# Wider, double-buffered conversion of the attention weights on two engines, and key transposes moved from the group stage to the chunk stage

## The chip, the cores and the metric

The program runs on the 8 cores of one Trainium2 chip, one sequence of the batch on each core, without communication between them. The metric is the device time of the slowest core in microseconds. The kernel before has a median of 5968.18 us over two runs (5965.78 and 5970.58).

## The reference

Each core computes one macaron layer for 2048 tokens of width 1024: half a feed-forward block, an attention block, and half a feed-forward block with the same weights again. Cut to what matters:

```python
x = x + 0.5 * ffn(layernorm(x), w_gate, w_up, w_down)
x = x + attn(layernorm(x), Wq, Wk, Wv, Wo, Wg1, Wg2, gamma, beta)
x = x + 0.5 * ffn(layernorm(x), w_gate, w_up, w_down)

def ffn(x, ...):      # every operand goes through a blockwise fp4 quantize-dequantize
    return fp4_linear(silu(fp4_linear(x, w_gate)) * fp4_linear(x, w_up), w_down)

def attn(x, ...):     # linear attention: no softmax, causal mask by multiplication
    q, k = lrpe(x @ Wq), lrpe(x @ Wk)            # silu, then rotary
    energy = einsum('bnhd,bmhd->bhnm', q, k) * tril
    out = einsum('bhnm,bmhd->bnhd', energy, x @ Wv)
    out = out * sigmoid(x @ Wg1 @ Wg2)
    return (layernorm(out) * gamma + beta) @ Wo
```

## The kernel before, in words

The program has four stages, with a barrier of all engines and all DMA counters (emit_phase_barrier, line 395) after the first, second and third.

**Weight preparation.** The activations x go into the SBUF tensor R (128 x 16384 fp32) once and stay there. The feed-forward weights are loaded, quantized on VectorE (DVE), transposed on TensorE (PE) into the PSUM tensor psW, evacuated by ScalarE (ACT) into evacW, and stored by DMAs that GpSimd (POOL) issues, into DRAM scratch tensors s_wgT, s_wuT, s_wdT. Then the four attention weights (q, k, v, o; 1024 x 1024 fp32 each) are only converted to bf16. This is the loop at lines 361 to 393: for each of four matrices and each of DK = 8 row blocks, SyncE (SP) loads a block of 128 x 1024 fp32 (512 KB) into wldA or wldB by turns (line 373), ACT casts it into one half of evacW (buf[:, 0:DM], 128 x 1024), and POOL issues the store of 256 KB to s_wq, s_wk, s_wv or s_wo (line 389). Two things set the order. The load waits for `sac.n`, the last ACT instruction emitted, so the load of block k waits for the cast of block k-1. The cast calls wait_stores, which waits for every store emitted so far (counters sgw, sgwd, sga), so cast k waits for store k-1 although it writes the other half of evacW:

```python
y.wait_ge(sac.h, sac.n)          # load k: the cast of block k-1
...
s.wait_ge(slot.h, ldm)           # cast k: its load
wait_stores(s)                   #         and all stores so far
```

**Feed-forward 1 and 2** (emit_ffn_call) read the scratch weights and work on four tiles of 128 tokens at a time. The diff does not touch them.

**Attention** (emit_attn). Work goes by groups g of GT = 2 chunks of 128 tokens, 8 groups in all; wbufA has three slots for weights, loaded by SP. The order in which instructions are emitted is the order of each engine's queue. For each group: sections(g); mixing(2g); epilogue(2g-1); o_load; emit_gate; mixing(2g+1); epilogue(2g).

sections(g) normalizes and transposes two tiles into xn_fm, then projects q and k in 8 steps each. A step is: PE matmuls into psA (line 748), ACT silu into qs_b, PE rotation matmul into psB (line 770), ACT copy into qp_b, and four DVE instructions that write qh or kh. After the last step of k, PE transposes kh for each of the two chunks, 16 instructions of 64 x 128 (line 817) into the one PSUM tensor psD, and DVE copies psD out (first chunk to ktm_sb, second chunk to the reused wkA). Then PE computes v for both chunks (line 852), with an ACT copy into v_g after each, and the small product with Wg1 (line 874).

mixing(c) runs four blocks of four heads: PE scores into psC (line 952), DVE multiplies by the mask into sTm, PE accumulates the output in psA from sTm and from the running state Sb (lines 979 and 983). Then PE multiplies the transposed keys with v_g into psB (line 1000), and DVE adds that to the fp32 state S32 and writes Sb. epilogue(c) is gate, layer norm, transposes, output projection (line 1099) and residual.

Each ACT block of instructions is preceded by an ACT_TABLE_LOAD, whatever its function. Vector and scalar instructions go through a helper, so that all have line 137; they are told apart by their tiles.

Of the kernel before, what the change touches and what calls it, by code (L numbers as in the profile page):

```python
# [9 lines left out]
BF16 = mybir.dt.bfloat16  # L10
# [15 lines left out]
GT = 2  # L26
# [11 lines left out]
def build_program():  # L38
# [70 lines left out]
    sga = Ctr("sga")  # L109
    sfg = [Ctr("sfg0"), Ctr("sfg1")]  # L110
# [7 lines left out]
    dma_ctrs = [ssu, slw[0], slw[1], sgw, sgwd, sga, sfg[0], sfg[1],  # L118
# [146 lines left out]
    def wait_stores(e):  # L265
        for ctr in (sgw, sgwd, sga):
            if ctr.n > 0:
                e.wait_ge(ctr.h, ctr.n)

    with ExitStack() as wes:  # L270
# [4 lines left out]
        evacW = WSB("evacW", [128, 2048], BF16)  # L275
# [3 lines left out]
        with nc.psum_tensor("psW", [128, 2048], BF16) as psW:  # L279
# [82 lines left out]

            for nm in ("q", "k", "v", "o"):
                dsrc, ddst = {"q": (dwq, s_att["q"]), "k": (dwk, s_att["k"]),
                              "v": (dwv, s_att["v"]), "o": (dwo, s_att["o"])}[nm]
                for k in range(DK):
                    buf = wldA if (k % 2 == 0) else wldB
                    pp = k % 2
                    slot = slw[k % 2]

                    def _(y, k=k, buf=buf, dsrc=dsrc):
# [7 lines left out]
                    def _(s, buf=buf, ldm=ldm, pp=pp, slot=slot):  # L379
# [4 lines left out]
                    S(_)  # L384
                    am = sac.n

                    def _(g, k=k, am=am, pp=pp, ddst=ddst):
                        g.wait_ge(sac.h, am)
                        g.dma_start(out=ddst[k * 128:(k + 1) * 128, :],
                                    in_=evacW[:, pp * 1024:(pp + 1) * 1024]).then_inc(sga.h, 16)  # L390
                    G(_)
                    sga.n += 16
            wprep_marks["attn"] = sga.n
# [243 lines left out]
    def emit_attn(rwaits):  # L637
        with ExitStack() as aes:
# [23 lines left out]
            with nc.psum_tensor("psA", [128, 2048], F32) as psA, \  # L662
# [10 lines left out]
                ktm_rd = {0: 0, 1: 0}  # L673
                ktm_b = {0: ktm_sb, 1: wkA[:, 0:512].bitcast(BF16)}
# [3 lines left out]
                def sections(g):  # L678
# [44 lines left out]
                    for nm, wp in (("q", 0), ("k", 1)):  # L723
                        def _(y, nm=nm, wp=wp, g=g, slot=sat[wp]):
                            y.wait_ge(spe.h, wsl_rd[wp])
                            if g == 0:
                                y.wait_ge(sga.h, wprep_marks["attn"])
# [79 lines left out]

                    qk_now = sdv.n
                    ctx["ktm_e"] = {}
                    for cl in range(GT):  # L810
                        def _(t_, cl=cl, qk_now=qk_now):
                            t_.wait_ge(sdv.h, qk_now)
                            t_.wait_ge(sdv.h, rs["psD_v"])
                            t_.wait_ge(sac.h, rs["psD_s"])
                            last = None
                            for hc in range(H):
                                last = t_.transpose(
                                    psD[:, hc * 64:(hc + 1) * 64],
                                    kh[:, hc * GTOK + cl * 128: hc * GTOK + (cl + 1) * 128],
                                    identb[0:64, 0:64])  # L820
                            spe.inc(last)
                        T(_)
                        ktt_m = spe.n

                        def _(v, cl=cl, ktt_m=ktt_m):
# [3 lines left out]
                        V(_)  # L829
                        ctx["ktm_e"][cl] = sdv.n  # L830
                        rs["psD_v"] = sdv.n
# [104 lines left out]
                def mixing(c):  # L936
# [55 lines left out]
                    def _(t_, cl=cl, ctx=ctx):  # L992
                        t_.wait_ge(sdv.h, ctx["ktm_e"][cl])
# [3 lines left out]
                        kts = ktm_b[cl]  # L997
                        last = None
                        for hc in range(H):
                            last = t_.matmul(psB[0:64, hc * 64:(hc + 1) * 64],  # L1000
                                             kts[:, hc * 64:(hc + 1) * 64],
# [5 lines left out]
                    ktm_rd[cl] = sup_m  # L1007
# [197 lines left out]
```

## Time and profile before

| what | us |
|---|---|
| median of the runs | 5968.18 |
| device time of the profiled execution | 5960.58 |
| span of its slowest core (core 5) | 5959.0 |
| spans of the eight cores | 5950.6 to 5959.0 |
| first load of the attention weights issued, and the feed-forward's first DVE instruction | 739.70, 972.62 |
| feed-forward 1, attention, feed-forward 2 (rounded edges) | 972 to 2690, 2690 to 4330, 4330 to 5959 |
| busy: PE, DVE, ACT, POOL | 1845.4, 2508.9, 1646.7, 384.2 |

Positions are microseconds from the start of the span of core 5. "Busy" is the time in which an engine executes. A row of the timeline reads: start, duration, engine, line, operation, output<-inputs, count, and in brackets the idle time ahead of it with what ended it. PEclk is the granted TensorE clock as a share of 2.4 GHz, so 0.50 is 1.2 GHz and 1.00 is 2.4 GHz.

### The profile page before, as it was taken

To read this page: it belongs to the slowest core of one execution; us is meant where nothing else is said; L and a number is where in the kernel's file an instruction comes from. 1 tells how busy PE (TensorE), PEld (TensorE's weight loads), DVE (VectorE), ACT (ScalarE), POOL (GpSimd) and SP (SyncE) were. 2 spreads that over 40 slices of the span, in tenths; PEclk is the share of its full clock that TensorE was granted. 3 is DMA by queue.
4 is the path that set the end of the run, shared out by engine and by line. 5 is a ranking of instruction groups with operands and counts; after the bars stand their busy time and mean duration, and the time that the engine had idled before them with its cause. 6 is when DMAs were issued, how large, how long until landed. Compare 5 with 4: busy or idle time off the path is not lost.

```text
span 5959.0 us, 36038 instructions; the slowest of 8 cores (5950.6 to 5959.0 us)
## 1 busy us (share of the span) xinstructions
PE 1845.4 (31%) x9264; PEld 924.1 (16%) x9264; DVE 2508.9 (42%) x3398; ACT 1646.7 (28%) x1718; POOL 384.2 (6%) x605
## 2 busy tenths in 40 slices
PE   0010100433333334423333333333323424344333
PEld 0000000211111111212211211211111212121111
DVE  7798602444535535322222222222246355354452
ACT  1222233222212212153342342242222223121220
POOL 3454500000000000000000000000000000000000
PEclk9999999776676666755555555555556766666667
DMA  4122132102020021110101101101011210220212
GB/s 148 67 76 78 60 109 85 53 25 67 25 64 29 25 64 53 36 57 29 49 23 43 57 15 43 57 15 43 29 34 48 64 28 25 64 53 27 65 25 92
DMA packets 209652, 304.60 MB, mean 51 GB/s; under 512 B 29808, under 2 KB 128112, under 8 KB 208432
## 3 DMA queue, kind: packets, MB, share of 16 engines
q1 hardware_dynamic: 184544, 256.98, 14.6%
q0 software_dynamic: 24912, 45.32, 2.1%
q8 instruction: 84, 1.38, 0.1%
q14 instruction: 112, 0.92, 0.1%
HBM read 268.11 MB, written 34.08 MB: 51 GB/s over the span
## 4 chain that ended last, share of the span: by engine, by line
DVE 29%; PE 27%; ACT 18%; issue 10%; DMA 9%; POOL 5%; DVEq 1%; ACTq 0%; POOLq 0%; SPq 0%
ACT L137 11%; PE psg L524 5%; PE psu L527 5%; PE psA L748 4%; DVE q_cF L137 4%; DMA wdb<-s_wdT 3%; PE psd L617 3%; DVE hb L137 3%; DVE q_iF L137 3%; DVE q_rF L137 3%; DVE q_bmF L137 3%; DVE wkD L137 2%; DVE btB L137 2%; POOL s_wdT L354 2%; ACT evacW L137 2%
## 5 line engine op out<-in xcount | busy, mean ns | idle before, releaser
L137 ACT ACT_TABLE_LOAD x815 | 1045.6, 1283 | 4204.5 <-PE pstB L572 1042.2
L524 PE MATMUL psg<-wgb,xq 128*128 128x512 bf16 (+1 forms) x1536 | 572.5, 381 | 39.3 <-ACT xq L137 21.7
L527 PE MATMUL psu<-wub,xq 128*128 128x512 bf16 (+1 forms) x1536 | 569.9, 380 | 0.0
L572 PE MATMUL pstB<-identb,btB 128*128 128x128 bf16 x704 | 90.2, 305 | 1158.1 <-DVE btB L137 1158.1
L137 DVE TENSOR_TENSOR hb<-wkA,psu 128x512 f32<-128x512 f32 (+1 forms) x192 | 123.5, 643 | 675.1 <-ACT wkA L137 675.1
L617 PE MATMUL psd<-wdb,hq 128*128 128x512 bf16 x1408 | 351.4, 398 | 106.9 <-DMA wdb<-s_wdT 85.3
L137 DVE TENSOR_TENSOR btB<-qs_b,cosr 128x256 bf16<-128x256 bf16 x128 | 37.4, 292 | 737.0 <-ACT qp_b L137 737.0
L1145 POOL DMA_DIRECT2D out<-R x16 | 8.4, 533 | 4953.7 <-DVE R L137 4953.7
L748 PE MATMUL psA<-xn_fm,wbufA 128*128 128x256 bf16 x1024 | 238.8, 413 | 277.4 <-ACT qp_b L137 255.0
L464 PE MATMUL pstA<-identb,btA 128*128 128x128 bf16 x256 | 32.4, 305 | 919.0 <-DVE btA L137 919.0
L333 PE MATMUL psW<-identb,wqb 128*128 128x128 bf16 x528 | 67.1, 306 | 665.3 <-ACT evacW L137 445.8
L572 PEld LDWEIGHTS pstB<-identb,btB 128*128 128x128 bf16 x704 | 67.4, 136 | 1184.7 <-issue 1184.7
L137 DVE SCALAR_TENSOR_TENSOR R<-psd,R 128x4096 f32<-128x4096 f32 x8 | 35.4, 4425 | 468.1 <-PE psd L617 468.1
L524 PEld LDWEIGHTS psg<-wgb,xq 128*128 128x128 bf16 x1536 | 156.9, 102 | 217.1 <-issue 80.0
L748 PEld LDWEIGHTS psA<-xn_fm,wbufA 128*128 128x128 bf16 x1024 | 132.2, 138 | 360.3 <-issue 311.4
L527 PEld LDWEIGHTS psu<-wub,xq 128*128 128x128 bf16 x1536 | 156.3, 102 | 169.2 <-issue 31.3
L617 PEld LDWEIGHTS psd<-wdb,hq 128*128 128x128 bf16 x1408 | 131.8, 101 | 324.7 <-issue 209.9
L464 PEld LDWEIGHTS pstA<-identb,btA 128*128 128x128 bf16 x256 | 24.7, 137 | 928.2 <-issue 928.2
L137 DVE TENSOR_REDUCE st_s<-R 128x4 f32<-128x4096 f32 (+1 forms) x9 | 52.6, 5842 | 269.0 <-DMA s_wo<-evacW 267.7
L137 DVE TENSOR_TENSOR sTm<-psC,mask 128x512 bf16<-128x512 f32 x64 | 44.2, 691 | 268.3 <-PE psC L952 267.4
L333 PEld LDWEIGHTS psW<-identb,wqb 128*128 128x128 bf16 x528 | 50.9, 137 | 681.2 <-issue 681.2
L137 DVE TENSOR_TENSOR q_cF<-q_iF,q_cF 128x1024 bf16<-128x1024 f32 (+1 forms) x128 | 148.2, 1158 | 13.7 <-DVE q_cF L137 0.5
(131 smaller groups left out, 3709.3 us busy)
## 6 DMA issues: line engine op xcount, KB each, us to landing
wdb<-s_wdT SPq DMA_DIRECT2D x176, 256.0 KB, 2.6
wgb<-s_wgT SPq DMA_DIRECT2D x320, 128.0 KB, 3.0
wub<-s_wuT SPq DMA_DIRECT2D x320, 128.0 KB, 3.1
wbufA<-s_wq SPq DMA_DIRECT2D x64, 256.0 KB, 7.8
wbufA<-s_wk SPq DMA_DIRECT2D x64, 256.0 KB, 9.1
wbufA<-s_wv SPq DMA_DIRECT2D x64, 256.0 KB, 4.5
wbufA<-s_wo SPq DMA_DIRECT2D x64, 256.0 KB, 5.4
R<-x POOLq DMA_DIRECT2D x16, 512.0 KB, 19.4
```

The source lines that it names most:

```text
L137: instr = f(*a, **kw)
L333: last = t.transpose(psW[:, pp * 1024 + s * 128: pp * 1024 + (s + 1) * 128], wqb[:, qb * FFI + (g0 + s) * 128: qb * FFI + (g0 + s + 1) * 128],
L354: g.dma_start(out=ddstT[c0 + s * 128: c0 + (s + 1) * 128, jcol * 128:(jcol + 1) * 128], in_=evacW[:, pp * 1024 + s * 128: pp * 1024 + (s + ...
L464: last = t_.transpose(pstA[:, pp * 1024 + k * 128: pp * 1024 + (k + 1) * 128], btA[:, pp * DM + k * 128: pp * DM + (k + 1) * 128], identb[:])
L524: t_.matmul(psg[:, pp * 512: pp * 512 + mw], lhs, wgbuf[:, wp * 4096 + k * 512: wp * 4096 + k * 512 + mw], start=(k == 0), stop=(k == DK - 1))
L527: last = t_.matmul(psu[:, pp * 512: pp * 512 + mw], lhs, wubuf[:, wp * 4096 + k * 512: wp * 4096 + k * 512 + mw], start=(k == 0), stop=(k ...
L572: last = t_.transpose(pstB[:, qpp * 1024 + sb * 128: qpp * 1024 + (sb + 1) * 128], btB[:, qpp * DM + sb * 128: qpp * DM + (sb + 1) * 128], ...
L617: last = t_.matmul(psd[:, j * 1024 + hf * 512: j * 1024 + (hf + 1) * 512], lhs, wdbuf[:, wp * DM + hf * 512: wp * DM + (hf + 1) * 512], st ...
L748: last = t_.matmul(psA[:, pp * 512: pp * 512 + GTOK], wbufA[:, wp * 8192 + k * 1024 + m * 128: wp * 8192 + k * 1024 + (m + 1) * 128], xn_f ...
L1145: g.dma_start(out=dout[t * TILE:(t + 1) * TILE, :], in_=Rt(t)).then_inc(sgo.h, 16)
```

## The change

Two parts.

**Attention weights.** The loop takes two row blocks at a time: 4 x 4 items instead of 4 x 8. A load carries 128 x 2 x 1024 fp32 (1 MB), a cast 128 x 2048, a store 512 KB; evacW grows from 2048 to 4096 columns, so each of two slots has its own 2048. Even items are cast by ACT as before, odd ones by DVE. The load of item ii waits for the cast of item ii-2 alone (the first two wait for the last DVE quantization). The cast waits for its load and for the stores of its own slot: the counter sga is split into sga and sga2. SP still issues all loads and POOL all stores, in order.

**Key transposes.** The transposes of kh and the DVE copy of psD leave sections(g) and go into mixing(c), between the last output matmul and the matmul that updates the state. Both chunks use ktm_sb; the second buffer and its waits are gone.

```diff
-        evacW = WSB("evacW", [128, 2048], BF16)
+        evacW = WSB("evacW", [128, 4096], BF16)
...
-                for k in range(DK):
-                    buf = wldA if (k % 2 == 0) else wldB
-                        y.wait_ge(sac.h, sac.n)
-                        y.dma_start(out=buf[:, 0:DM],
-                                    in_=dsrc[k * 128:(k + 1) * 128, :]).then_inc(slot.h, 16)
-                        s.wait_ge(slot.h, ldm)
-                        wait_stores(s)
-                        sac.inc(s.copy(evacW[:, pp * 1024:(pp + 1) * 1024],
-                                       buf[:, 0:DM]))
...
+                for k0 in range(0, DK, 2):
+                    ii = it2[0]
+                    it2[0] += 1
+                    buf = wldA if (ii % 2 == 0) else wldB
+                    pp = ii % 2
+                    sst = sgat[pp]
+                    use_v = (pp == 1)
+                        prev = cp_marks.get(ii - 2)
+                        if prev:
+                            y.wait_ge(prev[0].h, prev[1])
+                        else:
+                            y.wait_ge(sdv.h, sdv.n)
+                        y.dma_start(
+                            out=buf[:, 0:2 * DM].rearrange("p (t c) -> p t c", c=DM),
+                            in_=dsrc[k0 * 128:(k0 + 2) * 128, :]
+                            .rearrange("(t p) c -> p t c", p=128)).then_inc(slot.h, 16)
+                    def cpwaits(e, ldm=ldm, slot=slot, sst=sst):
+                        e.wait_ge(slot.h, ldm)
+                        for ctr in (sgw, sgwd, sst):
+                            if ctr.n > 0:
+                                e.wait_ge(ctr.h, ctr.n)
+                    if use_v:
+                            sdv.inc(v.tensor_copy(
+                                evacW[:, pp * 2048:(pp + 1) * 2048],
+                                buf[:, 0:2 * DM]))
+                    else:
+                            sac.inc(s.copy(
+                                evacW[:, pp * 2048:(pp + 1) * 2048],
+                                buf[:, 0:2 * DM]))
+                        g.wait_ge(cm[0].h, cm[1])
+                        g.dma_start(
+                            out=ddst[k0 * 128:(k0 + 2) * 128, :]
+                            .rearrange("(t p) c -> p t c", p=128),
+                            in_=evacW[:, pp * 2048:(pp + 1) * 2048]
+                            .rearrange("p (t c) -> p t c", c=DM)).then_inc(sst.h, 16)
```

In sections(g) this goes (with the 16 transposes of each chunk ahead of it):

```diff
-                            v.wait_ge(spe.h, ktt_m)
-                            v.wait_ge(spe.h, ktm_rd[cl])
-                            sdv.inc(v.tensor_copy(ktm_b[cl][:], psD[:]))
```

In mixing(c) this comes, after the last output matmul:

```diff
+                        t_.wait_ge(sdv.h, ctx["qk_m"])
+                        t_.wait_ge(sdv.h, rs["psD_v"])
+                        t_.wait_ge(sac.h, rs["psD_s"])
+                        last = None
+                        for hc in range(H):
+                            last = t_.transpose(
+                                psD[:, hc * 64:(hc + 1) * 64],
+                                kh[:, hc * GTOK + cl * 128: hc * GTOK + (cl + 1) * 128],
+                                identb[0:64, 0:64])
+                        spe.inc(last)
...
+                        v.wait_ge(spe.h, ktm_m)
+                        sdv.inc(v.tensor_copy(ktm_sb[:], psD[:]))
```

What SP's queue holds at the start of the attention weights, before (wldA and wldB are the load buffers; sac counts ACT's instructions, sdv DVE's):

```order
L373 DMA wldA<-wq 128x1024 [waits sac]
L375 UNCONDITIONAL_BRANCH
L373 DMA wldB<-wq 128x1024 [waits sac]
L375 UNCONDITIONAL_BRANCH
L373 DMA wldA<-wq 128x1024 [waits sac]
```

and now:

```order
L385 DMA wldA<-wq 128x2x1024 [waits sdv]
L389 UNCONDITIONAL_BRANCH
L385 DMA wldB<-wq 128x2x1024 [waits sdv]
L389 UNCONDITIONAL_BRANCH
L385 DMA wldA<-wq 128x2x1024 [waits sac]
L389 UNCONDITIONAL_BRANCH
L385 DMA wldB<-wq 128x2x1024 [waits sdv]
```

A load is twice as large, and loads to wldB now follow DVE instead of ACT.

On PE, at the end of the k projection of a group, before (line 770 is the last rotation matmul, line 852 the v projection):

```order
L770 MATMUL psB<-qs_b,p128t 128x256 [waits sac,sdv]
L822 UNCONDITIONAL_BRANCH
L817 MATMUL psD<-identb,kh 128x64 [waits sdv,sac]
L817 MATMUL psD<-identb,kh 128x64 x15
L822 UNCONDITIONAL_BRANCH
L817 MATMUL psD<-identb,kh 128x64 [waits sdv,sac]
L817 MATMUL psD<-identb,kh 128x64 x15
L857 UNCONDITIONAL_BRANCH
L852 MATMUL psA<-wbufA,xn_fm 128x512 [waits sat0,sac,sdv]
```

and now (lines 801 and 858 are the same two matmuls):

```order
L801 MATMUL psB<-qs_b,p128t 128x256 [waits sac,sdv]
L863 UNCONDITIONAL_BRANCH
L858 MATMUL psA<-wbufA,xn_fm 128x512 [waits sat0,sac,sdv]
L858 MATMUL psA<-wbufA,xn_fm 128x512 x15
```

The v projection follows the rotation matmul directly. At the end of a chunk's mixing, before (line 983 is the last output matmul, line 1000 the state update):

```order
L979 MATMUL psA<-v_g,sTm 128x64
L983 MATMUL psA<-Sb,qh 128x64
L1005 UNCONDITIONAL_BRANCH
L1000 MATMUL psB<-v_g,ktm_sb 64x64 [waits sdv,sac]
L1000 MATMUL psB<-v_g,ktm_sb 64x64 x15
```

and now (lines 989 and 1026):

```order
L985 MATMUL psA<-v_g,sTm 128x64
L989 MATMUL psA<-Sb,qh 128x64
L1009 UNCONDITIONAL_BRANCH
L1004 MATMUL psD<-identb,kh 128x64 [waits sdv,sac]
L1004 MATMUL psD<-identb,kh 128x64 x15
L1031 UNCONDITIONAL_BRANCH
L1026 MATMUL psB<-v_g,ktm_sb 64x64 [waits sdv,sac]
L1026 MATMUL psB<-v_g,ktm_sb 64x64 x15
```

The 16 transposes now stand between the output matmuls and the state update, once per chunk; the DVE copy that stands between them waits for the one and releases the other.

## Rows read from the trace of the kernel before

**Rows 1.** The page: the chain that ended last, by engine, and the granted clock by slices

```profile
DVE 29%; PE 27%; ACT 18%; issue 10%; DMA 9%; POOL 5%; DVEq 1%; ACTq 0%; POOLq 0%; SPq 0%
PEclk9999999776676666755555555555556766666667
```

**Rows 2.** Timeline, two steps of the attention weights' conversion

```profile
745.04 1.28 ACT L137 ACT_TABLE_LOAD   x1 [5.41 <-DMA s_wdT<-evacW]
746.33 1.04 ACT L137 CAST evacW<-wldA 128x1024 bf16<-128x1024 f32 x1
...
751.91 1.28 ACT L137 ACT_TABLE_LOAD   x1 [4.54 <-DMA s_wq<-evacW]
...
972.62 4.42 DVE L137 TENSOR_REDUCE st_s<-R 128x4 f32<-128x4096 f32 x1 [267.67 <-DMA s_wo<-evacW]
```

**Rows 3.** Busy time by stretch: engines, then granted clock, DMA share, GB/s

```profile
10.00:40.00 30.00, 0.00 (x0) 0.00 (x0) 27.58 (x24) 0.00 (x0) 5.23 (x10) 1.00 1.00 333
745.00:972.00 227.00, 0.00 (x0) 0.00 (x0) 0.00 (x0) 74.50 (x64) 17.29 (x32) 1.00 0.36 109
```

**Rows 4.** DMA issues of the whole run: queue, count, KB each, median us to landing

```profile
wldA<-wgate SPq DMA_DIRECT2D x6, 1024.0 KB, 6.1
...
s_wgT<-evacW POOLq DMA_DIRECT2D x176, 32.0 KB, 1.8
```

**Rows 5.** Tile R before 745 us: the 16 loads of x, 512 KB each

```profile
L245 POOL DMA_DIRECT2D R<-x x16: 546/563/667, 1.6 to 9.5; - x16
...
DMA to landing us min/median/max: 11.3/19.4/30.4
```

**Rows 6.** Groups by shape, feed-forward weights (100 to 740) and attention (2690 to 4330)

```profile
L137 DVE TENSOR_SCALAR q_rW<-wldA 128x2048 bf16<-128x2048 f32 x10 | 12.3, 1227 | 1.1
...
L137 ACT CAST qp_b<-psB 128x256 bf16<-128x256 f32 x114 | 42.5, 372 | 1.3
```

**Rows 7.** Timeline, end of the k projection of the first group and its v projection

```profile
2696.73 0.37 ACT L137 CAST qp_b<-psB 128x256 bf16<-128x256 f32 x1
...
2698.13 0.68 DVE L137 TENSOR_TENSOR kh<-btB 64x256 bf16<-64x256 bf16 x2
...
2699.16 1.01 PE L817 MATMUL psD<-identb,kh 64*128 64x64 bf16 x16 [3.92 <-DVE kh L137]
2700.41 0.69 DVE L137 COPY ktm_sb<-psD 128x1024 bf16<-128x1024 bf16 x1 [1.61 <-PE psD L817]
...
2701.36 1.00 PE L817 MATMUL psD<-identb,kh 64*128 64x64 bf16 x16 [1.19 <-DVE ktm_sb L137]
...
2702.29 5.31 PE L852 MATMUL psA<-wbufA,xn_fm 128*128 128x512 bf16 x16
```

**Rows 8.** Timeline, end of the first chunk's mixing

```profile
2733.28 1.06 PE L1000 MATMUL psB<-v_g,ktm_sb 128*64 128x64 bf16 x16
2734.58 1.21 DVE L137 TENSOR_TENSOR S<-S,psB 64x1024 f32<-64x1024 f32 x1 [2.96 <-PE psB L1000]
```

**Rows 9.** Busy time by stretch: columns as in rows 3, around v, and by stage

```profile
2699.00:2705.60 6.60, 5.25 (x40) 2.94 (x41) 1.38 (x2) 0.00 (x0) 0.00 (x0) 0.50 0.00 0
2705.60:2708.00 2.40, 2.00 (x9) 0.72 (x7) 0.00 (x0) 0.26 (x1) 0.00 (x0) 0.97 0.00 0
972.00:2690.00 1718.00, 603.74 (x2871) 285.83 (x2871) 758.94 (x1094) 470.50 (x498) 0.00 (x0) 0.68 0.16 46
4330.00:5959.00 1629.00, 578.21 (x2760) 271.39 (x2760) 736.89 (x1047) 391.88 (x398) 8.39 (x16) 0.67 0.17 48
```

**Rows 10.** Timeline, GpSimd's issue of eight stores of s_wdT, twice

```profile
527.72 4.25 POOL L354 DMA_DIRECT2D s_wdT<-evacW  x8 [12.59 <-ACT evacW L137]
...
558.37 7.80 POOL L354 DMA_DIRECT2D s_wdT<-evacW  x8 [8.37 <-ACT evacW L137]
560.04 1.63 DVE L137 TENSOR_SCALAR q_iW<-q_iW 128x2816 int32<-128x2816 int32 x1
```

**Rows 11.** Tile v_g: the copies of the v projection, two per group

```profile
L137 ACT CAST v_g<-psA x16: 1012/1012/1013, 2709.0 to 4247.7; 128x1024 bf16<-128x1024 f32 x16
```

More of the change, by code:

```diff
@@ L109, in build_program @@
     sga = Ctr("sga")
+    sga2 = Ctr("sga2")
+    sgat = [sga, sga2]
     sfg = [Ctr("sfg0"), Ctr("sfg1")]
@@ L265, in wait_stores @@
     def wait_stores(e):
-        for ctr in (sgw, sgwd, sga):
+        for ctr in (sgw, sgwd, sga, sga2):
             if ctr.n > 0:
@@ L361, in build_program @@
                 wprep_marks[name] = sst.n
+            it2 = [0]
+            cp_marks = {}
             for nm in ("q", "k", "v", "o"):
@@ L365, in build_program, with _ @@
                               "v": (dwv, s_att["v"]), "o": (dwo, s_att["o"])}[nm]
-                for k in range(DK):
-                    buf = wldA if (k % 2 == 0) else wldB
-                    pp = k % 2
-                    slot = slw[k % 2]
-                    def _(y, k=k, buf=buf, dsrc=dsrc):
-                        y.wait_ge(sac.h, sac.n)
-                        y.dma_start(out=buf[:, 0:DM],
-                                    in_=dsrc[k * 128:(k + 1) * 128, :]).then_inc(slot.h, 16)
+                for k0 in range(0, DK, 2):
[3 more added lines that the diff above has]
+                    pp = ii % 2
+                    slot = slw[pp]
+                    sst = sgat[pp]
+                    use_v = (pp == 1)
+                    def _(y, k0=k0, buf=buf, dsrc=dsrc, ii=ii, slot=slot):
+                        prev = cp_marks.get(ii - 2)
[7 more added lines that the diff above has]
+                            .rearrange("(t p) c -> p t c", p=128)).then_inc(slot.h, 16)
                     Y(_)
@@ L391, in build_program, with _ @@
-                    G(_)
-                    sga.n += 16
-            wprep_marks["attn"] = sga.n
+                    def cpwaits(e, ldm=ldm, slot=slot, sst=sst):
[4 more added lines that the diff above has]
+                    if use_v:
+                        def _(v, pp=pp, buf=buf):
+                            cpwaits(v)
+                            sdv.inc(v.tensor_copy(
+                                evacW[:, pp * 2048:(pp + 1) * 2048],
+                                buf[:, 0:2 * DM]))
+                        V(_)
+                        cp_marks[ii] = (sdv, sdv.n)
+                    else:
+                        def _(s, pp=pp, buf=buf):
+                            cpwaits(s)
+                            sac.inc(s.copy(
+                                evacW[:, pp * 2048:(pp + 1) * 2048],
+                                buf[:, 0:2 * DM]))
+                        S(_)
+                        cp_marks[ii] = (sac, sac.n)
@@ L395, in emit_phase_barrier @@
+                    sst.n += 16
+            wprep_marks["attn"] = (sgat[0].n, sgat[1].n)
     def emit_phase_barrier():
@@ L726, in _ @@
                             if g == 0:
-                                y.wait_ge(sga.h, wprep_marks["attn"])
+                                y.wait_ge(sga.h, wprep_marks["attn"][0])
+                                y.wait_ge(sga2.h, wprep_marks["attn"][1])
                             for k in range(DK):
@@ L806, in sections @@
                     wsl_rd[1] = projpe["k"]
[L808 to L825, printed above, removed]
-                            v.wait_ge(spe.h, ktt_m)
-                            v.wait_ge(spe.h, ktm_rd[cl])
-                            sdv.inc(v.tensor_copy(ktm_b[cl][:], psD[:]))
-                        V(_)
-                        ctx["ktm_e"][cl] = sdv.n
-                        rs["psD_v"] = sdv.n
                     def _(y, g=g, slot=sat[0]):
@@ L992, in _ @@
                     def _(t_, cl=cl, ctx=ctx):
-                        t_.wait_ge(sdv.h, ctx["ktm_e"][cl])
+                        t_.wait_ge(sdv.h, ctx["qk_m"])
[8 more added lines that the diff above has]
+                        spe.inc(last)
+                    T(_)
+                    ktm_m = spe.n
+                    def _(v, ktm_m=ktm_m):
+                        v.wait_ge(spe.h, ktm_m)
+                        sdv.inc(v.tensor_copy(ktm_sb[:], psD[:]))
+                    V(_)
+                    ktme_m = sdv.n
+                    rs["psD_v"] = ktme_m
+                    def _(t_, cl=cl, ktme_m=ktme_m, ctx=ctx):
+                        t_.wait_ge(sdv.h, ktme_m)
                         t_.wait_ge(sac.h, ctx["v_m"])
@@ L1000, in _ @@
                             last = t_.matmul(psB[0:64, hc * 64:(hc + 1) * 64],
-                                             kts[:, hc * 64:(hc + 1) * 64],
+                                             ktm_sb[:, hc * 64:(hc + 1) * 64],
                                              v_g[:, cl * DM + hc * 64: cl * DM + (hc + 1) * 64],
```

15 lines of the change are left out of this document (3 added, 12 removed).

## The prediction

> **What bounds the kernel now.** I read the page's chain first [rows 1]: DVE 29%, PE 27%, ACT 18%, DMA 9%, POOL 5%. No engine is the bound alone; the end is set by hand-overs, so what a step costs is its length on the chain of its stage. The 9% of DMA and 5% of POOL are transfers and their issue that something waited for. The timeline says where: after the last store of the feed-forward weights every step of the attention weights' conversion has one shape [rows 2]. Two 512 KB blocks never overlap. ACT idles 4.54 us for the store of the block before, loads its table (1.28), casts (1.04), and only then are the next load and this block's store issued (SP waits for the cast, front section). 32 such steps fill the time from 745.04 to the barrier at about 972.4, 227.4 us or 7.1 us each; DVE waits 267.67 us for the end of it [rows 2]. All of it is on the chain, and in it the DMA engines are busy only 36% [rows 3]: the stage is bound by latency, not by bytes. In attention each group is a serial hand-over between PE, ACT and DVE, so single pieces of 1 or 2 us count there as well.
>
> **The attention weights.** The bytes are the same: 32 x 512 KB read, 32 x 256 KB written, 25.2 MB.
>
> Removed: 32 serial steps, 227.4 us.
>
> Put in their place: 8 rounds, in each of which slot A (ACT) and slot B (DVE) do a load of 1 MB, a cast of 128 x 2048 and a store of 512 KB. The pieces:
> - DVE cast: the same form of output, input and width took 1.23 us as a tensor_scalar [rows 6].
> - ACT cast: 1.04 us for 1024 columns [rows 2], 0.37 for 256 [rows 6], so 0.88 ns per column and 1.94 us for 2048; with the table load 3.2 us.
> - DMA at full load: 109 GB/s at a share of 0.36 is 303 GB/s at a share of 1; a stretch of loads alone, with every DMA engine busy, moved 333 [rows 3]. The first has the mix of loads and stores that stays, in rows of 1024 elements as before, so I take 303.
> - Landing: a load of 1 MB took 6.1 us, a store of 32 KB 1.8 [rows 4], so about 1.8 us of a transfer is fixed.
>
> By latency alone slot A's round would be 6.1 + 3.2 + 0.1 for the hand-over = 9.4 us. By bytes a round is 3.15 MB / 303 GB/s = 10.4 us. The bytes decide, if the two slots' transfers fill each other's gaps. They do if transfers of one queue land one after the other rather than together. The 16 loads of x say so: issued within 8 us, they landed after 11.3 to 30.4 us, not all at the end [rows 5]. So A's load lands about halfway through a round, ACT casts for 3.2 us while B's transfers still flow, and B's cast runs while A's new ones do.
>
> Sum from 745.04 on: the first two loads are there already (they may now start after the last quantization, 267.67 us before 972.62, at 705). ACT's first cast with its issue takes 3.2 + 0.7 = 3.9 us. Then the rest of the bytes, 25.2 less 2.1 of the first two loads, is 23.1 MB at 303 GB/s, 76 us. I add 0.9 us in each of 7 rounds for gaps that the overlap leaves, half of the fixed 1.8, and 3 us at the end for the last DVE cast and the landing of its store. 3.9 + 76 + 6 + 3 = 89 us, so 138 are saved. The early pair of loads, 2.1 MB or some 7 us of full DMA, meets one or two stores of s_wdT that are on the chain. That costs between nothing and all of its 7 us; I take 2, since the stores' packets come between the loads' ones: net 136.
>
> Bounds: at 333 GB/s with no gaps it is 3.9 + 69 + 3 = 76, a saving of 151. With no overlap at all between a round's transfers and its casts, a round is 10.4 + 1.8 + 3.2 + 0.5 = 15.9, and 7 rounds with start and end 111 + 3.9 + 7 = 122, a saving of 105. I stay near the first since the landing rows speak for overlap.
>
> **The key transposes out of sections.** The first v matmul started at 2702.29 to 2702.36, behind both chunks' transposes and a DVE copy [rows 7]. Its other waits are older: the last qp_b copy ended at 2697.10, and PE follows an engine by 0.26 us (the copy to ktm_sb ended at 2701.10, the next transposes began at 2701.36 [rows 7]). The qp_b copy's end is 2696.73 + 0.37. So v starts at 2697.36, 5.0 us earlier, in each of 8 groups: 40 us. What is late next is v itself; DVE finishes kh at 2698.81 as before [rows 7], long before the scores need it.
>
> One loss is hidden in it. In this stretch PE ran at a granted 0.50 (1.2 GHz) and came to 0.97 (2.4 GHz) at 2705.6, about halfway through the first v batch, after 6.4 us in which transposes and v followed each other [rows 9]. Without transposes ahead, the rise may come no earlier in the batch or later. The batch took 5.31 us [rows 7]; all at 1.2 GHz, 16 x 512 columns is 6.8. So it costs between 0 and 1.5 us in each group. I take 0.4, nearer to the first, since v is itself most of the work ahead of the rise: 3 us in all.
>
> **The key transposes into mixing.** Before, the update matmuls followed the output matmuls at once (2733.28) and DVE waited 2.96 us for them with nothing else queued [rows 8]. Now PE transposes, DVE copies, PE goes on: 2701.36 - 2699.16 = 2.2 us by the very same pieces [rows 7], all in line. Behind the waiting copy in DVE's queue stands the state update, then the epilogue; nothing passes it. In 16 chunks this is 35 us. Nothing stands beside it that could hide it, and the other marks that the transposes wait for (psD, kh) are old by then, so I give it 0.2 us either way: 32 to 38 us.
>
> Attention in sum: -40 + 3 + 35 = -2 us, between -8 and +10.
>
> **Sum.** 5960.6 (the profiled execution) - 136 - 2 = 5822.6. The median of the runs shown stands 7.6 us above that execution, 0.13%; I take part of this in and say 5825 us, 2.4% below the median. A measurement of this kernel can tell about 2% from no change, that is 119 us, so faster than 5849 counts as faster.
>
> **Rivals.**
> - *Lockstep.* The two slots' transfers share the engines and land together, so both casts stand in the open: the upper bound above, a saving of 105 and 2, 5854 us. For it: both slots' first transfers are issued within a microsecond. Against it: the landing times of x. Chance 0.10.
> - *The descriptor stall.* While DVE worked on SBUF operands with one tensor input, eight store issues of GpSimd took 7.80 us instead of 4.25 [rows 10], so an issue can be held by a DVE instruction of that kind. The new DVE cast is one, and its 1.23 us can hold the store of the other slot once a round: 8 x 1.2 = 10 us, 5835 us. Chance 0.10. The Trainium skill's page "SBUF — State Buffer" (section "Who interferes with whom") says that DVE casts in a two-port mode and GpSimd's descriptor writes exclude each other for the whole instruction. The trace agrees with a slowdown, 7.80 against 4.25, and by that rule this rival's 10 us would be the ceiling. Before the change no DVE work ran in this stage.
> - *v does not move.* Something other than the transposes holds the v projection, for instance a wait that the trace hides behind them. Then the 40 us do not come and 35 are added: 5865 us. Against it: SP asks for v's weights once the q projection is done, eight steps of the k projection earlier. Chance 0.03.
> - *The clock is paid back.* PE is idle through the whole conversion with its clock granted in full [rows 3], the slices fall to 0.7 and less right behind it [rows 1], and in the feed-forward stages it is granted 0.68 and 0.67 with 604 + 578 = 1182 us of PE busy time [rows 9]. If a shorter rest lowers the grant, the feed-forwards pay. It decides from 1182 x (0.68 / c - 1) = 138, c = 0.61. At 0.50 in both stages it costs 425 us: 6248 us, slower. Against it: the grant in feed-forward 2, long after any rest, is the same as in feed-forward 1. Chance 0.01.
>
> **How the numbers follow.** The forecast has 0.76. Faster by over 2% holds for the forecast and the stall; the worst of the forecast's own spread: 0.76 + 0.10 = 0.86. Within 2%, with lockstep and v: 0.10 + 0.03 = 0.13. Slower: 0.01. The range is 5804 to 5853: the low end is the bound of 151 with attention at -6, the high end just reaches the lockstep case's edge.
>
> **What would show it.** In the changed profile the stretch from the first attention-weight cast to the first instruction of feed-forward 1 should be 85 to 95 us long with a DMA share of 0.85 to 0.95, and successive ACT casts 10.5 to 12 us apart. Lockstep would show spacings near 16 and a share near 0.65. The stall would show as store issues of GpSimd over 1.5 us long. In attention the v matmuls should begin 0.3 us after the last qp_b copy, the update matmuls 2.2 us after the last output matmul, and the group's period, (4247.7 - 2709.0 less the 6.3 between a group's two copies) / 7 = 219 us [rows 11], should change by less than 1 us. The granted clock of both feed-forward stages should stay at 0.67 to 0.68; if it falls below 0.61 the forecast is wrong in sign. If the period of a group grows by 4 us or more, the v step failed.

## The result, and the profile after

The changed kernel has a median of 5848.14 us (5838.01 to 5886.59, 9 runs) against 5969.09 us before (8 runs): a ratio of 0.9805, with a 95% interval of 0.9774 to 0.9836. It is faster, by 1.6 to 2.3%; whether by more than the 2% that the forecast named, the interval leaves open. The forecast was 5825 us, in a range of 5804 to 5853, so the time lies inside the range, 23 us above the point and 5 us below the upper end. In the profiled execution cores 4 to 7 ran for 267 to 420 us of the feed-forward stages at a granted clock of 0.81, a level that cores 0 to 3 never show there and that four cores of the run with the old conversion show too, so all comparisons below are of cores 0 to 3, unless others are named.

First the answer to [rows 1], the page of the slowest core after:

```profile
DVE 29%; PE 28%; ACT 18%; issue 10%; DMA 8%; POOL 5%; DVEq 1%; ACTq 0%; SPq 0%; POOLq 0%
```

The shares hardly move, although over 120 us are gone; a chain by engine does not find a stage. The times between fixed points of the program do. They are means over cores 0 to 3, from the first DVE instruction of feed-forward 1 and from the first and last ACT copy of v:

| stretch, us | before | after |
|---|---|---|
| start to feed-forward 1 | 965.1 | 839.7 |
| feed-forward 1, to the first copy of v | 1736.4 | 1734.0 |
| attention, first to last copy of v | 1538.8 | 1539.4 |
| from there to the end | 1713.5 | 1717.9 |

The whole gain, 125 us, lies ahead of feed-forward 1. Attention did not change. The two other stages differ by -2 and +4.

The timeline of core 0 of the changed kernel, two rounds of the conversion, answers to [rows 2]:

```profile
755.45 1.28 ACT L139 ACT_TABLE_LOAD   x1 [8.91 <-DMA s_wq<-evacW]
756.74 1.90 ACT L139 CAST evacW<-wldA 128x2048 bf16<-128x2048 f32 x1
757.41 1.23 DVE L139 CAST evacW<-wldB 128x2048 bf16<-128x2048 f32 x1 [12.80 <-DMA s_wq<-evacW]
758.73 0.37 SPq L385 DMA_DIRECT2D wldA<-wk  x1
759.18 1.42 POOL L418 DMA_DIRECT2D s_wq<-evacW  x2 [10.66 <-ACT evacW L139]
759.60 0.37 SPq L385 DMA_DIRECT2D wldB<-wk  x1
767.37 1.28 ACT L139 ACT_TABLE_LOAD   x1 [8.72 <-DMA s_wq<-evacW]
```

The two casts cost what was worked out (1.90 and 1.23 us). But both fall into the same 3 us, and all four transfers of a round are issued within 2 us of each other. ACT then waits 8.7 us, and not for its load: the row says that a store ended the wait. The DMA issues of that core from 744 us on show which lands first (columns: queue, count, KB, median us to landing):

```profile
s_wk<-evacW POOLq DMA_DIRECT2D x4, 512.0 KB, 8.9
wldA<-wv SPq DMA_DIRECT2D x2, 1024.0 KB, 6.2
wldB<-wv SPq DMA_DIRECT2D x2, 1024.0 KB, 10.2
```

Slot A's load is there after 6.2 us, but its cast writes the buffer that the store of two items back still reads, and that takes 8.9. All seven waits of ACT between its casts end with a store. Slot B waits for its load, 10.2, in five of its seven rounds, and for its store in the other two, of which the rows above show one. So the slots run nearly in step. The busy time of the same core in a stretch of the conversion answers to [rows 3] (columns as there; the last three are granted clock, DMA share, GB/s):

```profile
760.00:825.00 65.00, 0.00 (x0) 0.00 (x0) 6.14 (x5) 15.90 (x10) 8.09 (x11) 1.00 0.77 264
```

The DMA engines are busy 77% (68 to 77% over the eight cores), where 85 to 95% was expected and 36% was the share before. 264 GB/s at a share of 0.77 is 343 GB/s at full share.

In attention, the end of a chunk's mixing answers to [rows 7, 8]:

```profile
2595.60 1.04 PE L1004 MATMUL psD<-identb,kh 64*128 64x64 bf16 x16
2596.81 0.69 DVE L139 COPY ktm_sb<-psD 128x1024 bf16<-128x1024 bf16 x1 [2.76 <-PE psD L1004]
...
2597.97 1.03 PE L1026 MATMUL psB<-v_g,ktm_sb 128*64 128x64 bf16 x16 [1.34 <-DVE ktm_sb L139]
2599.25 1.21 DVE L139 TENSOR_TENSOR S<-S,psB 64x1024 f32<-64x1024 f32 x1 [1.75 <-PE psB L1026]
```

The update stands 2.37 us behind the transposes (2.2 forecast). At the other end, the first v batch follows the last rotation copy (2565.27 + 0.37) by 0.25 us, as forecast:

```profile
2565.27 0.37 ACT L139 CAST qp_b<-psB 128x256 bf16<-128x256 f32 x1
...
2565.89 5.23 PE L858 MATMUL psA<-wbufA,xn_fm 128*128 128x512 bf16 x16 [2.11 <-ACT qp_b L139]
```

So both steps happened, 5.0 us gained per group and 2.37 lost per chunk, and over 8 groups and 16 chunks the sum is 40 against 38. The period of a group is 219.0 us as a mean over all cores, as before.

### The profile page after: what moved, and what is told of

Same layout as the page of the kernel before. It is cut to its first block, busy times and chain, and to the rows that moved or that the text cites. A ratio compares the mean times of both kernels' runs of the same rounds, so it can differ in the third digit from the quotient of the medians.

```text
span 5885.1 us, 35854 instructions; the slowest of 8 cores (5828.3 to 5885.1 us)
## 1 busy us (share of the span) xinstructions
PE 1909.0 (32%) x9264; PEld 936.8 (16%) x9264; DVE 2518.3 (43%) x3406; ACT 1597.8 (27%) x1670; POOL 379.1 (6%) x589
## 4 chain that ended last, share of the span: by engine, by line
DVE 29%; PE 28%; ACT 18%; issue 10%; DMA 8%; POOL 5%; DVEq 1%; ACTq 0%; SPq 0%; POOLq 0%
ACT L139 11%; PE psg L556 6%; PE psu L559 6%; PE psA L779 4%; DVE q_cF L139 4%; PE psd L649 4%; DMA wdb<-s_wdT 4%; DVE hb L139 3%; DVE q_iF L139 3%; DVE q_rF L139 3%; DVE q_bmF L139 3%; DVE wkD L139 2%; DVE btB L139 2%; POOL s_wdT L356 2%; DVE q_ivF L139 2%
## 5 line engine op out<-in xcount | busy, mean ns | idle before, releaser
L556 PE MATMUL psg<-wgb,xq 128*128 128x512 bf16 (+1 forms) x1536 | 591.7, 393 | 38.8 <-ACT xq L139 21.3
L559 PE MATMUL psu<-wub,xq 128*128 128x512 bf16 (+1 forms) x1536 | 588.8, 392 | 0.0
L649 PE MATMUL psd<-wdb,hq 128*128 128x512 bf16 x1408 | 377.6, 422 | 101.4 <-DMA wdb<-s_wdT 80.7
L139 DVE TENSOR_REDUCE q_bmF<-hb 128x64 f32<-128x1024 f32 (+1 forms) x96 | 108.5, 1131 | 102.2 <-PE pstB L604 99.7
```

Source lines behind the costliest of these rows:

```text
L139: instr = f(*a, **kw)
L556: t_.matmul(psg[:, pp * 512: pp * 512 + mw], lhs, wgbuf[:, wp * 4096 + k * 512: wp * 4096 + k * 512 + mw], start=(k == 0), stop=(k == DK - 1))
L559: last = t_.matmul(psu[:, pp * 512: pp * 512 + mw], lhs, wubuf[:, wp * 4096 + k * 512: wp * 4096 + k * 512 + mw], start=(k == 0), stop=(k ...
L649: last = t_.matmul(psd[:, j * 1024 + hf * 512: j * 1024 + (hf + 1) * 512], lhs, wdbuf[:, wp * DM + hf * 512: wp * DM + (hf + 1) * 512], st ...
```

## Experiments

For the conversion I give two numbers from each profile, means over all eight cores: the stage, from the start of ACT's first cast of attention weights to feed-forward 1, and the lead, from the end of the last quantization to that first cast. Before they are 226.0 and 40.6 us, after 94.9 and 43.1. The time ahead of the last quantization also varies by a few us from run to run and from core to core; no part of the change touches it. Ratios are against the kernel before in the same rounds, whose median differs from one set of rounds to the next, so the variants are compared by their stages.

**One part at a time.** The first run has the new conversion and attention as before, with the transposes in sections and two buffers:

```diff
-                        sdv.inc(v.tensor_copy(ktm_sb[:], psD[:]))
...
+                            v.wait_ge(spe.h, ktm_rd[cl])
+                            sdv.inc(v.tensor_copy(ktm_b[cl][:], psD[:]))
```

> The attention-weight conversion of the changed kernel with the key transposes left in the group stage. Theory (the whole gain is the conversion, the key move is worth nothing): 5840 to 5850 us, as the changed kernel; copies of v from first to last 1539 us apart. Rival (the key move costs the 35 us in mixing and gives less than 40 back): faster than the changed kernel by 10 us or more. On the clock: if one die's granted clock still lies some 0.007 under the other's in several runs, that comes with the conversion or from outside, not with the key move.

Measured: 5854.31 us against 5988.03 for the kernel before in these rounds, ratio 0.9753 (0.9709 to 0.9796). Stage 95.1, lead 42.8; v's first to last copy 1538 to 1542 us.

The second run is the reverse: the conversion as before and the changed attention.

```diff
-                for k0 in range(0, DK, 2):
+                for k in range(DK):
...
-                                y.wait_ge(sga2.h, wprep_marks["attn"][1])
```

> The key transposes moved, the conversion as before. Theory: 5967 us, within 4 us of the kernel before; the first v matmul 5.0 us earlier behind the last rotation copy, 2.2 us more ahead of each state update. Rival (only one of the two is true): 35 to 40 us slower or faster. If here too a die's clock lies lower than the other's in several runs, while the kernel before does not show it, it comes with the key move.

Measured: 5988.45 us against 5988.03, ratio 0.9991 (0.9958 to 1.0023). Stage 226.7, lead 40.5; v's copies 1540 to 1544 us. The theory holds on both sides: the conversion carries the whole gain, the key move is worth nothing within 4 us (attention is 3.6 us longer here than before, as a mean over the cores).

**Is DVE's cast worth anything, or does it hold GpSimd?**

```diff
-                    use_v = (pp == 1)
+                    use_v = False
```

> The changed kernel with every cast on ACT, nothing on DVE in the conversion. Theory (DMA transfers and their landing set the round, and DVE's cast stands beside them): the conversion is longer by 0 to 2 us per round of two blocks, since ACT's second cast with its table load takes 3.2 us in place of 1.23, stage 98 to 115 us. Rival (DVE holds GpSimd's store issues): store issues get shorter and the conversion not longer.

Measured: 5850.99 us in one run; stage 93.7, lead 42.0. The second engine gave nothing: with all casts on ACT the stage is 1.2 us shorter, where 98 to 115 us was expected. The casts now stand one behind the other, and the slots are 4 to 5 us apart; that this pays for the slower cast is argued, not shown. The timeline of core 0:

```profile
748.82 0.71 POOL L418 DMA_DIRECT2D s_wq<-evacW  x1 [6.21 <-ACT evacW L139]
749.31 1.28 ACT L139 ACT_TABLE_LOAD   x1 [1.03 <-DMA s_wq<-evacW]
750.61 1.90 ACT L139 CAST evacW<-wldB 128x2048 bf16<-128x2048 f32 x1
```

All 128 store issues by GpSimd on the eight cores take 0.71 to 0.73 us here, beside no DVE cast. In the changed kernel 39 of 128 run beside a cast on DVE. Core 0 has the second-longest of them, and in the next round one that is not lengthened:

```profile
770.65 1.23 DVE L139 CAST evacW<-wldB 128x2048 bf16<-128x2048 f32 x1 [12.02 <-DMA wldB<-wk]
771.10 0.93 POOL L418 DMA_DIRECT2D s_wk<-evacW  x1 [10.49 <-ACT evacW L139]
...
782.41 1.23 DVE L139 CAST evacW<-wldB 128x2048 bf16<-128x2048 f32 x1 [10.52 <-DMA s_wk<-evacW]
783.17 0.71 POOL L418 DMA_DIRECT2D s_wk<-evacW  x1 [10.02 <-ACT evacW L139]
```

None of the 39 ends less than 0.14 us after the cast beside it; 14 of them are longer than 0.73 us, and the longest is 0.94. So the descriptor stall exists, at 0.23 us at most and not at 1.2 us a round. Every one of these issues starts 0.43 us or more after its cast, and the times fit an issue that cannot finish before the cast does: only what is left of the cast holds it. The Trainium skill's page "SBUF — State Buffer" (section "Who interferes with whom") says that the one that comes first has the shared ports for its whole instruction and the other is blocked; by that, as an estimate, an issue could be held for up to 1.2 us. The trace agrees, with 0.94 against 0.71, but no issue here came at a cast's start.

**What the early first loads cost.**

```diff
-                            y.wait_ge(sdv.h, sdv.n)
+                            y.wait_ge(sac.h, sac0)
```

Here sac0 is ACT's count ahead of the loop.

> The changed kernel with the first two loads after the last evacuation of the down weights, as before, in place of after the last quantization. Theory (the early 2 MB cost one store's landing on the chain): the last evacuations run 3 to 4 us earlier, but both first loads now land 7 to 10 us after them, so the conversion ends 4 to 6 us later. Rival (the early loads are free): no change ahead of 745 us, later by 7 or more after it.

Measured: 5836.55 us in one run; lead 44.1 and stage 93.7, where the changed kernel has 43.1 and 94.9. The last evacuation of the down weights ends 2.5 us earlier, where 3 to 4 was expected, and the first cast follows it after 9.9 us in place of 6.3, means over all cores. With the stage's 1.2 us the two together differ by 0.2 us, where 4 to 6 was expected. In this one run the place of the first loads does not matter.

**Size or overlap.**

```diff
-                for k0 in range(0, DK, 2):
+                for k0 in range(DK):
...
-                            out=buf[:, 0:2 * DM].rearrange("p (t c) -> p t c", c=DM),
+                            out=buf[:, 0:DM].rearrange("p (t c) -> p t c", c=DM),
```

Casts and stores shrink with it, to 1024 columns and 256 KB.

> The changed kernel's waits, two slots and two engines, with blocks of 512 KB again (16 rounds of two in place of 8). Theory (a round is the bytes at about 340 GB/s, 4.7 us per 1.57 MB, plus some 3.5 us that the overlap leaves open, whatever the size): rounds of 7.5 to 9 us, the conversion 125 to 140 us, so about 90 of the 125 us come from overlap and the rest from the size. Rival (bytes alone decide): rounds of 6.4, the conversion as with 1 MB blocks.

Measured: 5892.96 us in one run; stage 143.4, lead 40.7. The rounds are 9.1 us and the stage 143.4, both just above the expectation:

```profile
766.14 1.28 ACT L139 ACT_TABLE_LOAD   x1 [6.93 <-DMA s_wq<-evacW]
766.73 0.69 DVE L139 CAST evacW<-wldB 128x1024 bf16<-128x1024 f32 x1 [7.54 <-DMA s_wq<-evacW]
...
775.25 1.28 ACT L139 ACT_TABLE_LOAD   x1 [6.77 <-DMA s_wq<-evacW]
775.87 0.69 DVE L139 CAST evacW<-wldB 128x1024 bf16<-128x1024 f32 x1 [8.45 <-DMA s_wq<-evacW]
```

A round moves 1.57 MB here, 4.6 us at 343 GB/s, so 4.5 us are open, as against 2.8 with blocks of 1 MB. In these rows a store ends both engines' waits. Of the 131 us by which the conversion got shorter, the waits, the second slot and the second engine give 83 and the block size 48.

**Four output buffers.** Casts go by turns to two slots of evacW and two of wqb, which is idle by then, each with a counter of its own:

```diff
-                    sst = sgat[pp]
+                    so = ii % 4
+                    sst = sgat4[so]
+                    ob = (evacW[:, so * 2048:(so + 1) * 2048] if so < 2
+                          else wqb[:, (so - 2) * FFI:(so - 2) * FFI + 2048])
```

> The changed kernel with four buffers for the casts' output (two in evacW, two in the idle wqb) and four counters, so a cast waits for the store four items back and no longer for the one two back. Theory (ACT's cast is late because its slot's last store lands after its load, 9.1 against 7.0 us): ACT casts 10 to 11.5 us apart in place of 12.8, the conversion 10 to 15 us shorter. Rival (the DMA engines' rate decides, the order of landing does not): rounds stay at 12.5 or more.

Measured: 5845.85 us, ratio 0.9759 (0.9705 to 0.9813), the same as the changed kernel's within its interval; in the profile the stage is 82.6 us, 12.3 shorter, with a lead of 42.3. The timeline of core 0:

```profile
763.34 1.28 ACT L142 ACT_TABLE_LOAD   x1 [7.71 <-DMA wldA<-wq]
...
768.16 1.23 DVE L142 CAST wqb<-wldB 128x2048 bf16<-128x2048 f32 x1 [14.45 <-DMA wldB<-wq]
...
774.05 1.28 ACT L142 ACT_TABLE_LOAD   x1 [7.52 <-DMA wldA<-wk]
...
779.12 1.23 DVE L142 CAST evacW<-wldB 128x2048 bf16<-128x2048 f32 x1 [9.74 <-DMA wldB<-wk]
```

Now the loads end both engines' waits, DVE's cast stands 5 us behind ACT's start, half a round as the forecast had it, and ACT's spacing is 10.7 us here. This is the overlap that I had assumed, and it needed the output buffers. The median does not show the 12 us: in this profile attention is 1545.8 us as a mean over the cores, 5.5 longer than in the changed kernel's, and the v batches take 0.6 us more per group.

**Four input buffers as well.**

```diff
-                        prev = cp_marks.get(ii - 2)
+                        prev = cp_marks.get(ii - 4)
```

The third buffer is new, the fourth a scratch tensor of the quantization.

> Four output buffers as in the last experiment, and four input buffers as well (wldA, wldB, one new, one in a scratch tensor of the quantization), so a load waits for the cast four items back. Theory (only bytes are left: 25.2 MB at 330 to 350 GB/s): DMA share above 0.9, ACT casts 9.3 to 9.8 us apart, the conversion 70 to 80 us. Rival (the queues' order or the memory holds it): no faster than with four output buffers alone.

Measured: 5841.77 us in one run; stage 74.8, lead 42.3. The windows of core 0, first this kernel, then the one with four output buffers:

```profile
745.00:815.00 70.00, 0.00 (x0) 0.00 (x0) 8.47 (x7) 22.26 (x14) 10.75 (x15) 1.00 0.96 322
```

```profile
760.00:825.00 65.00, 0.00 (x0) 0.00 (x0) 7.37 (x6) 20.92 (x14) 8.57 (x12) 1.00 0.95 316
```

At a share of 0.96 the stage is bound by its bytes. 74.8 us from the first cast are 76.1 from its table load, and the lower bound of the prediction was 76. At 322 GB/s with a share of 0.96 the rate at full share is 335 GB/s, near the bound's 333.

**Key transposes where PE waits anyway.** The new conversion, and in sections one chunk's transposes behind each v batch:

```diff
+                        def _(t_, c=c, qk_now=qk_now):
+                            t_.wait_ge(sdv.h, qk_now)
...
+                                last = t_.transpose(
+                                    psD[:, hc * 64:(hc + 1) * 64],
+                                    kh[:, hc * GTOK + c * 128: hc * GTOK + (c + 1) * 128],
+                                    identb[0:64, 0:64])
```

> The conversion of the changed kernel; the key transposes in the group stage again, but one chunk's behind each of the two v batches, where PE waits 2.7 us for ACT's copy of v. Theory (the key work costs only where it stands alone on the chain; 5 us per group gained by v's early start, nothing paid in mixing): 35 to 40 us faster than the changed kernel, group period 214 us. Rival (the later v batch or the Wg1 product is pushed back by the transposes and the granted clock): under 15 us faster.

Measured: 5837.5 us, ratio 0.9728 (0.9678 to 0.9777); attention, first to last copy of v, is 1512.8 us as a mean over the cores, 27 under the changed kernel, and the group's period 215.0. That is between the two expectations; the medians are only 11 us apart. v still comes 5 us earlier per group, and mixing no longer pays 2.37 us per chunk, so 14 x 2.37 = 33 us were due in the seven periods. The 5 or 6 that are missing are in PE's own batches. The groups of attention by shape, of core 4 of this kernel (busy us and mean ns of one matmul after the first bar):

```profile
L1132 PE MATMUL psA<-wbufA,y_fm 128*128 128x512 bf16 x256 | 86.3, 512 | 19.7 <-DVE y_fm L139 19.7
L863 PE MATMUL psA<-wbufA,xn_fm 128*128 128x512 bf16 x256 | 84.6, 504 | 34.2 <-ACT qp_b L139 17.2 <-ACT v_g L139 17.0
```

and of core 0 of the changed kernel:

```profile
L1124 PE MATMUL psA<-wbufA,y_fm 128*128 128x512 bf16 x256 | 94.1, 548 | 19.6 <-DVE y_fm L139 19.6
L858 PE MATMUL psA<-wbufA,xn_fm 128*128 128x512 bf16 x256 | 68.9, 430 | 38.8 <-ACT v_g L139 21.5 <-ACT qp_b L139 17.3
...
L906 PE MATMUL psB<-wg2b,xg1g 64*128 64x512 bf16 x32 | 12.9, 493 | 23.7 <-ACT gate_sb L139 21.2 <-DVE Sb L139 2.5
...
L880 PE MATMUL psC<-xn_fm,wg1b 128*64 128x256 bf16 x64 | 8.3, 272 | 21.6 <-ACT v_g L139 21.6
```

The v batches of this core take 16 us more than those of core 0 of the changed kernel (84.6 against 68.9), and the output projections 8 us less (86.3 against 94.1). Single cores scatter: v takes 78.0 us on core 5 of the changed kernel. So the account goes by means over the eight cores: a group's v and Wg1 batches take 1.67 us more here, and the stretch from its first scores to the next projection is 5.72 us shorter, of which 4.74 are the transposes with their copy and 0.98 mostly the output projections and the gate's product. In seven periods that is 12 us lost and 7 gained beside the 33. In most groups v's two batches take 6.3 and 5.2 us here, and 5.0 and 3.6 there. The work is the same; what differs is where the grant rises from 0.50 to 1.00. In the changed kernel it rises within the first batch and is still 1.00 when the second starts; where the second takes 5.2 us here, the first had its rise near its end, the grant was back at 0.50 when the second started, and it rose once more within it.

**Both together.**

Four buffers on both sides of the cast, and the transposes as in the last run:

```diff
-                        prev = cp_marks.get(ii - 2)
+                        prev = cp_marks.get(ii - 4)
...
+                            sdv.inc(v.tensor_copy(ktm_b[c][:], psD[:]))
```

> Four input and four output buffers in the conversion, and one chunk's key transposes behind each v batch. Theory (the two savings lie in different stages and add up: 20 us from the conversion, 27 from attention): 47 us under the changed kernel, 5790 to 5795 us on undisturbed cores. Rival (attention's saving depends on where the granted clock rises and does not carry over): 20 to 30 us under it.

Measured: 5786.14 us (5780.0 to 5871.33, 4 runs), ratio 0.9694 (0.9675 to 0.9713). The kernel before has 5971.63 in these rounds. Stage 74.2, lead 41.8, attention 1512.7: both savings carry over. This beats both kernels, by 3.1% and about 1%. It is also more than was expected: 62 us under the changed kernel's median instead of 47, and cores 0 to 3 are 65 us under that kernel's. The two savings are 48 of these 65; another 13 lie in the feed-forward stages (1729.7 and 1708.9 us), which no part of the change touches, and why is open.

**Both chunks' transposes behind the second v batch.**

The same blocks, in a loop of their own behind that of the v batches:

```diff
+                    ctx["v_m"] = sac.n
+                    wsl_rd[0] = spe.n
+
+                    for c in range(GT):
                         def _(t_, c=c, qk_now=qk_now):
...
-                    ctx["v_m"] = sac.n
-                    wsl_rd[0] = spe.n
```

> As the run beside it, but both chunks' key transposes behind the second v batch. Theory (each v batch is short only if PE comes to it without transposes between the batches; the wait there for ACT's copy of v is 2.7 us and the two transposes with a DVE copy between take 3.1, so 0.5 us sticks out per group): the second v batch 3.61 us in all groups, group period no more than 1 us longer than in the run beside it or up to 2 us shorter. Rival (the order of transposes and v batches does not matter to the clock): second batches of 5.2 us here too, period 0.5 us longer.

Measured: 5813.52 us, ratio 0.9725 (0.9682 to 0.9768); cores 4 to 7 5764 to 5778 us against 5757 to 5778 for all eight in the run beside it, and v's copies on these four 1512.9 us apart, against 1512.6. But the second v batch takes 5.2 us in most groups here too. My theory that the transposes between the batches keep it slow has fallen: with none between them it is as slow. The period is 215.0 us, 0.1 longer than in the run beside it. What sets the place where the clock rises is open.

## Why the prediction was right, and where it was off

**The 32 serial steps go, 227 us; 8 rounds take their place.** Right. With half the change undone, the conversion alone makes the gain, and the lead grew by 2.5 us for the early loads (2 forecast).

**The round.** Forecast 89 us from the first table load, measured 93.1 on core 0 (743.34 to 836.47); on all cores the stage from the first cast is 94.9 where the forecast's is 88. Two terms were off, in opposite directions, so that the sum is nearer than its terms, which is luck. The DMA engines at full share move 343 GB/s here and not 303: a round's bytes take 9.2 us, not 10.4. And the overlap leaves 2.8 us of each round open (12.0 us between ACT's table loads, 9.2 of bytes), not 0.9; as a mean over all cores the casts are 12.4 us apart, above the 10.5 to 12 that was to show the forecast. The step that failed inside a forecast that came true is "A's load lands about halfway through a round, ACT casts while B's transfers still flow". The load does land halfway, but ACT's cast waits for the store of its own slot, and the sum never asked when that lands. It lands at 8.9 us, late enough to bring both slots nearly into step. The run with four output buffers shows it: without this wait the stage is 82.6 us, better than the forecast.

**Lockstep and the stall.** The lockstep rival was half true: the slots do run nearly together, but at 12.0 us a round and not 15.9, since slot B's transfers still flow while ACT works. The stall was not worth its 10 us: no issue took over 0.94 us, and the run without DVE's cast is 1.2 us shorter in the stage.

**v earlier.** Right: 5.0 us a group. The same groups of core 0 before, by shape:

```profile
L1099 PE MATMUL psA<-wbufA,y_fm 128*128 128x512 bf16 x256 | 83.7, 499 | 19.8 <-DVE y_fm L137 19.8
L852 PE MATMUL psA<-wbufA,xn_fm 128*128 128x512 bf16 x256 | 77.2, 469 | 21.5 <-ACT v_g L137 21.5
...
L874 PE MATMUL psC<-xn_fm,wg1b 128*64 128x256 bf16 x64 | 13.4, 381 | 21.8 <-ACT v_g L137 21.8
...
L900 PE MATMUL psB<-wg2b,xg1g 64*128 64x512 bf16 x32 | 10.3, 405 | 24.0 <-ACT gate_sb L137 21.5 <-DVE Sb L137 2.5
```

On this core v went from 77.2 to 68.9 us and the product with Wg1 from 13.4 to 8.3, 13 us in all. But it is the core with the largest change: as means over the eight, a group's two v batches went from 9.26 to 9.11 us and the product from 1.75 to 1.06. So the clock term, charged at 3 us for v, is -1 us in eight groups, and with the product, which stood in no term, 7 us are gained.

**Transposes in mixing.** 2.37 us, not 2.2, so 38 us instead of 35. A second cost stood in no term: on core 0 the output projections went from 83.7 to 94.1 us and the gate's from 10.3 to 12.9, 13 us in all, again by the place where the grant rises. It comes with the key move: on core 4 the projections take 83.7 us with the conversion alone and 93.9 with the key move alone. As means over the eight cores, the stretch from a group's first scores to the next projection is 6.0 us longer, 4.74 for the transposes and 1.26 for such batches. In the seven periods between v's copies that makes -35 for v's start, -6 for its batches and Wg1's, +33 and +9, so +1 us; +1.4 was measured on all eight cores and +0.6 on cores 0 to 3. The forecast of -2 was right by luck, with two clock terms that largely cancel, of which it had a part of one, with the wrong sign.

**The clock in the feed-forwards.** It was not paid back. It did not answer to the shorter rest on cores 0 to 3 (0.689 to 0.691 for the whole run, 0.697 before, over a span that lost 125 us at full grant). The stretches take 1734 and 1718 us against 1736 and 1714.

**The sum.** Against its own execution the forecast was 138 us less; cores 0 to 3 lost 122.8 (means of 5953.8 and 5831.0). Of the 15.2 us between, 7.8 are the stage, 2.8 the time ahead of the last quantization, 2.6 attention, and 2.0 the two feed-forward stretches. The median of 5848 is one of slowest cores, and stands 17 us above that mean of four.

## What to carry to other kernels

A double buffer has two ends: when loads are set free to run ahead, look at when the store of the same slot lands, since the output buffer is the next thing that a cast waits for. Splitting work between two engines gives nothing while transfers set the pace; here buffers did, 20 us of them, and the second engine 0. Work that must be inserted into a serial chain belongs where its engine already waits for another one: the same transposes cost 38 us in one place and, behind the v batches, left attention 27 us shorter.

## What was not expected of the hardware

The same matmuls changed their length by their place alone. A batch of 16 x 512 columns took 3.6 us at a grant of 1.00 and between 4.4 and 6.6 us when part of it ran at 0.50, and moving 1 us of transposes elsewhere changed which batches of a group were short: v's second one took 3.6 us in most groups of the changed kernel and 5.2 in most groups of the kernels with the transposes back in sections and mixing free of them. And a store issue by GpSimd beside a DVE cast looked held only for what was left of the cast: none of 39 ended less than 0.14 us after it.
